# Batch 1's maximum and exponential moved into the first batch's FFN steps, with four small reorderings ahead of them

## The reference

```python
x = L0_attn_x                                   # (8, 512, 128) float32
x = x + _layernorm(_L0_attn_ref(_layernorm(x), gamma, beta, w_qkv, w_out, b_out))
x = x + _layernorm(_L0_ffn_ref(_layernorm(x), Wg, Wu, Wd))

# _L0_attn_ref: layernorm, q, k, v = xn @ w_qkv in 4 heads of 32
k = jax.nn.softmax(k, axis=1)                   # over the 512 tokens, per channel
context = jnp.einsum('bnhd,bnhe->bhde', k, v)
out = jnp.einsum('bhde,bnhd->bnhe', context, q * DIM_HEAD ** -0.5)
return out.reshape(b, n, 128) @ w_out + b_out + x

# _L0_ffn_ref: the sum over 8 experts, with hidden size 512
acc += (silu(x @ wg) * (x @ wu)) @ wd
```

## Time and profile before

| | before |
|---|---|
| three runs | 546.48, 546.70, 546.71 us; median 546.7 |
| the profiled execution | 546.29 us |
| its span in the profile | 544.5 us |
| TensorE busy | 536.6 us, 99% of the span |
| VectorE, ScalarE, GpSimd busy | 443.0, 345.5, 163.4 us |
| TensorE clock granted in the front and in the first steps | 1.00 of full speed |

### The profile page before, as it was taken

The page is one execution under the profiler, slowest core; times in us unless marked ns, Lnnn a source line. Parts: engine busy times, 40 slices in busy tenths (PEclk is TensorE's granted clock), DMA queues, the critical chain, the costliest instruction groups (busy, mean ns, idle before and its releaser), DMA issues.

```text
span 544.5 us, 8689 instructions
## 1 busy us (share of the span) xinstructions
PE 536.6 (99%) x2596; PEld 462.0 (85%) x2596; DVE 443.0 (81%) x987; ACT 345.5 (63%) x630; POOL 163.4 (30%) x211
## 2 busy tenths in 40 slices
PE   9899999999999999999999999999999999999996
PEld 5688888888888888888888888888888888888885
DVE  6796986989778897798978898688986889778666
ACT  5886877556675566755667566665667555655554
POOL 5697770305303171032601235021350005001001
PEclk9999999999999999999999999999999999999999
DMA  7254110220111201202012021020210210110000
GB/s 217 79 156 134 41 58 1 78 77 21 60 39 41 96 6 54 67 11 98 27 32 78 17 82 59 0 79 31 67 39 1 78 59 1 39 40 1 20 1 19
DMA packets 34081, 28.68 MB, mean 53 GB/s; under 512 B 3697, under 2 KB 25970, under 8 KB 34034
## 3 DMA queue, kind: packets, MB, share of 16 engines
q1 hardware_dynamic: 32736, 27.47, 15.9%
q10 hardware_dynamic: 1298, 0.66, 0.4%
HBM read 17.37 MB, written 10.75 MB: 52 GB/s over the span
## 4 chain that ended last, share of the span: by engine, by line
PE 97%; DVE 1%; DMA 0%; POOL 0%; issue 0%; SPq 0%; POOLq 0%; DVEq 0%; ACT 0%
PE acc_att_ps L1180 11%; PE acc_att_ps L1183 11%; PE acc_att_ps L1181 11%; PE gate_ps L1180 10%; PE gate_ps L1183 10%; PE gate_ps L1181 10%; PE up_ps L1180 10%; PE up_ps L1183 10%; PE up_ps L1181 10%; PE acc_att_ps L1226 1%; DMA wqkv<-in_L_attn_w_qkv_dram 0%; PE acc_att_ps L1214 0%; PE acc_att_ps L1234 0%; PE acc_att_ps L1335 0%; PE gate_ps L1415 0%
## 5 line engine op out<-in xcount | busy, mean ns | idle before, releaser
L715 ACT ACTIVATE gs<-gate_ps 128x512 f32<-128x512 f32 x255 | 152.0, 596 | 173.9 <-PE gate_ps L1183 171.6
L973 DVE TENSOR_TENSOR h<-gs,up_ps 128x512 f32<-128x512 f32 x231 | 157.7, 683 | 81.7 <-PE up_ps L1183 79.1
L960 DVE TENSOR_TENSOR h_lo<-h,h_hi 128x512 fp32r<-128x512 f32 x231 | 172.7, 748 | 0.2
L692 ACT ACTIVATE h_hi<-h 128x512 fp32r<-128x512 f32 x231 | 143.9, 623 | 7.7 <-DVE h L973 7.2
L1180 PE MATMUL gate_ps<-x1nT_hi,wg_hi 128*128 128x512 f32 (+1 forms) x254 | 98.0, 386 | 0.0
L1183 PE MATMUL acc_att_ps<-h_lo,wd_hi 128*128 128x512 f32 (+1 forms) x256 | 96.9, 379 | 0.0
L1180 PE MATMUL acc_att_ps<-h_hi,wd_hi 128*128 128x512 f32 (+1 forms) x256 | 96.9, 379 | 0.0
L1181 PE MATMUL acc_att_ps<-h_hi,wd_lo 128*128 128x512 f32 (+1 forms) x256 | 96.8, 378 | 0.0
L1180 PE MATMUL up_ps<-x1nT_hi,wu_hi 128*128 128x512 f32 (+1 forms) x254 | 96.2, 379 | 0.0
L1181 PE MATMUL up_ps<-x1nT_hi,wu_lo 128*128 128x512 f32 (+1 forms) x254 | 96.1, 378 | 0.0
L1181 PE MATMUL gate_ps<-x1nT_hi,wg_lo 128*128 128x512 f32 (+1 forms) x254 | 96.1, 378 | 0.0
(11 more groups left out here) (246 smaller groups left out, 535.4 us busy)
## 6 DMA issues: line engine op xcount, KB each, us to landing
w_raw<-in_L_ffn_Wg_dram SPq DMA_DIRECT2D x8, 256.0 KB, 3.1
w_raw<-in_L_ffn_Wu_dram SPq DMA_DIRECT2D x8, 256.0 KB, 3.0
w_raw<-in_L_ffn_Wd_dram SPq DMA_DIRECT2D x8, 256.0 KB, 2.9
x_in<-in_L_attn_x_dram SPq DMA_DIRECT2D x7, 256.0 KB, 2.9
t_dram_x1n<-t_blk_x1n SPq DMA_DIRECT2D x7, 256.0 KB, 2.0
t_out_x1n<-t_dram_x1n SPq DMA_DIRECT2D x28, 64.0 KB, 2.0
t_dram_acc<-t_blk_acc SPq DMA_DIRECT2D x7, 256.0 KB, 2.3
t_out_acc<-t_dram_acc SPq DMA_DIRECT2D x28, 64.0 KB, 2.0
```

The source lines that it names most:

```text
L692: act.activation(h_hi[s % NH][:, :], h_of(t, s)[:, :], ACT.Copy).then_inc(s_hhi, 1)
L715: act.activation(gs[q][:, :], gate_ps[q][:, :], ACT.Silu).then_inc(s_silu, 1)
L960: dve.tensor_tensor(h_lo[s % NH][:, :], h_of(t, s)[:, :], h_hi[s % NH][:, :].bitcast(F32), ALU.subtract).then_inc(s_hlo, 1)
L973: dve.tensor_tensor(h_of(t, s)[:, :], gs[q][:, :], up_ps[q][:, :], ALU.mult).then_inc(s_h, 1)
```

## The change

Five edits, all in the front and in batch 0's steps:

1. VectorE's `kmax` of batch 1 moves from the front to the beginning of step 3, and ScalarE's `exp` to the end of step 4. `E_T` and `E_store` follow one step later each, and the weight splits of steps 3 to 6 are moved out of the way: `split_hi(6)` into the front, `split_hi(8)` from step 5 to step 7 and those up to m = 17 one or two steps later than before; `split_lo` follows.
2. The load of silu's table moves ahead of `first_n(1)`'s copy in the front. As the exponential now stands in step 4, the program gains two loads there: exp's ahead of it and silu's behind it.
3. TensorE makes the second half's transposes (`first_n(1)`) before the first `early_low`, not after it.
4. `b_out`'s product moves from between `first_kT` and `first_k` to behind A, and takes 128 rows (a row of b_out and 127 of zeros that a new memset on VectorE writes) in place of one. VectorE's `kmax_diag` no longer waits for it; `first_yb(0)` does, and stands behind the copy of A.
5. `first_U(2)` moves ahead of `first_kT`.

```diff
-FIRST_DVE = {"E_T": 4, "next_stats": 8, "A": 12, "M": 14, "z": 17, "z_stats": 17, "next_T": 19, "wk_lo": 20,
+FIRST_DVE = {"kmax": 3, "E_T": 5, "next_stats": 8, "A": 12, "M": 14, "z": 17, "z_stats": 17, "next_T": 19, "wk_lo": 20,
-FIRST_ACT = {"E_store": 5, "E_load": 8, "G": 16, "wk_hi": 18, "next_xnT": 26, "next_xnT_hi": 27, "x1n_hi": 30}
+FIRST_ACT = {"exp": 4, "E_store": 6, "E_load": 8, "G": 16, "wk_hi": 18, "next_xnT": 26, "next_xnT_hi": 27, "x1n_hi": 30}
-HI_AT = {6: 2, 7: 3, 8: 5, 9: 6, 10: 7, 11: 8, 12: 9, 13: 11, 14: 12, 15: 13, 16: 14, 17: 15, 18: 17, 19: 18, 20: 19,
+HI_AT = {7: 2, 8: 7, 9: 8, 10: 9, 11: 10, 12: 11, 13: 12, 14: 13, 15: 14, 16: 15, 17: 16, 18: 17, 19: 18, 20: 19,
          21: 21, 22: 22, 23: 23}
-LO_AT = {5: 1, **{m: when + 1 for m, when in HI_AT.items()}}
+LO_AT = {5: 1, 6: 3, 7: 4, **{m: when + 1 for m, when in HI_AT.items() if m > 7}}
...
+        b_row = sb("b_row", [P, D])
...
+            act.wait_ge(s_b_zero, 1)
+            act.dma_start(b_row[0:1, :], b_out.rearrange("(a d) -> a d", a=1)).then_inc(s_b_row, 16)
...
-            act.wait_ge(s_f_erec, 1)
-            attention("exp", 1, 1, True)
+            act.wait_ge(s_mask, 3)
+            act.activation(silu_warm[:, :], zcol[:, :], ACT.Silu)
             act.wait_ge(s_f_n, 2)
             act.activation(blocks_of(x1nT_hi[0][:, :], 1), two(acc_ps[:, REST]), ACT.Copy).then_inc(s_x1nT_hi, 1)
-            act.wait_ge(s_mask, 3)
-            act.activation(silu_warm[:, :], zcol[:, :], ACT.Silu)
+            split_hi(6)
...
-            dve.wait_ge(s_bout_ps, 1)
...
+            dve.wait_ge(s_f_A_ps, 1)
+            dve.tensor_copy(A_sb[:, :], gate_ps[0][:, 0:D]).then_inc(s_f_A, 1)
+            dve.wait_ge(s_bout_ps, 1)
             dve.wait_ge(s_wvT, HEADS)
             first_yb(0)
-            dve.wait_ge(s_f_A_ps, 1)
-            dve.tensor_copy(A_sb[:, :], gate_ps[0][:, 0:D]).then_inc(s_f_A, 1)
...
-            dve.wait_ge(s_f_esum, 1)
-            attention("kmax", 1, 1, True)
...
+            first_U(2)
             pe.wait_ge(s_f_xnT, 1)
             first_kT(0, HALF)
...
-            pe.matmul(up_ps[2][:, D:2 * D], ones[0:1, :].bitcast(F32), b_row[:, :], start=True,
-                      stop=True).then_inc(s_bout_ps, 1)
...
-            first_U(2)
             first_U(3)
...
             last.then_inc(s_f_A_ps, 1)
+            pe.wait_ge(s_b_row, 16)
+            pe.wait_ge(s_U_half, 1)
+            pe.matmul(up_ps[2][:, D:2 * D], ones[:, :].bitcast(F32), b_row[:, :], start=True,
+                      stop=True).then_inc(s_bout_ps, 1)
...
             pe.wait_ge(s_f_lo, 1)
-            early_low(0, 0)
             first_n(1)
-            for s in range(1, EARLY):
+            for s in range(EARLY):
                 early_low(s, 0)
```

More of the change, by code:

```diff
@@ L111, in build @@
         bout_bc = sb("bout_bc", [P, D])
-        b_row = sb("b_row", [1, D])
+        b_row = sb("b_row", [P, D])
         wqkv = sb("wqkv", [P, 3 * D])
@@ L227, in build @@
         s_bout = sem("s_bout")
+        s_b_zero = sem("s_b_zero")
         s_b_row = sem("s_b_row")
@@ L654, in attention @@
                     if first:
+                        act.wait_ge(s_f_erec, 1)
                         act.activation(ET[:, :], att_ps[:, :], ACT.Exp, bias=kmax_neg[:, 0:1], scale=1.0,
@@ L725, in _ @@
             act.dma_start(bcol[:, :], beta[0].rearrange("a d -> d a")).then_inc(s_gb, 16)
-            act.dma_start(b_row[:, :], b_out.rearrange("(a d) -> a d", a=1)).then_inc(s_b_row, 16)
+            act.wait_ge(s_b_zero, 1)
+            act.dma_start(b_row[0:1, :], b_out.rearrange("(a d) -> a d", a=1)).then_inc(s_b_row, 16)
             act.wait_ge(s_w_ps, 1)
@@ L861, in attention @@
                     dve.wait_ge(s_kT_ps, c)
+                    if first:
+                        dve.wait_ge(s_f_esum, 1)
                     dve.tensor_reduce(kmax_neg[:, 0:1], att_ps[:, :], AX_X, ALU.max, negate=True).then_inc(s_kmax, 1)
@@ L997, in _ @@
             dve.memset(warm[:, :], 0.0).then_inc(s_warm, 1)
+            dve.memset(b_row[:, :], 0.0).then_inc(s_b_zero, 1)
             dve.memset(head_mask[:, :], 0.0).then_inc(s_mask, 1)
@@ L1359, in _ @@
             first_kT(1, REST)
-            pe.wait_ge(s_mask, 4)
-            pe.wait_ge(s_b_row, 16)
-            pe.wait_ge(s_U_half, 1)
-            pe.matmul(up_ps[2][:, D:2 * D], ones[0:1, :].bitcast(F32), b_row[:, :], start=True,
-                      stop=True).then_inc(s_bout_ps, 1)
             first_k(0)
             first_k(1)
+            pe.wait_ge(s_mask, 4)
             pe.wait_ge(s_f_kdiag, 1)
```

## The result

The changed kernel takes 549.55 us in the median of six runs (548.47 to 550.81), the kernel before beside it 546.59: a ratio of 1.0055 with an interval of 1.0036 to 1.0074. The forecast was 547.3, at most 548.1. The runs of the changed kernel stand in two groups, three near 548.5 and three near 550.6. The profiled run is one of the first group: 548.51 us, with a span of 546.7 against 544.5.

A forecast was written before the change was run, and what follows sets the result against it. TensorE, busy 99% of the span, was taken as the bound. Terms -0.05, -0.22, -0.45, +0.75, +0.38 and +0.2 summed to +0.6 us: 546.9 on the profiled execution, 547.3 as median, range 546.0 to 548.1 (0.80).

The forecast's parts named there:

- the one that carries VectorE in step 4: Steps around batch 0's step 4: engines carried forward by row distances; waits of +0.75, +0.38 and +0.2 us followed.
- the one collision: VectorE's h_lo(1) against GpSimd's wd_lo: not side by side, so h_lo(1) runs 25.8 to 26.4, about 1.4 us.
- The front to `through_heads`: Front: quicker kmax_diag wins 0.25 us, b_out's product behind A costs 0.22, U's product 0.02; -0.05 in all.
- the product of 128 rows: b_out's product behind A in the front: taken as 0.22 us, the shape of A's, against 0.41 for one row.
- The second half's first product: End of the front: first_n(1)'s transposes come sooner, -0.22 us; this product moves from 21.23 to 20.96.
- Silu's table: Step 0: the load runs earlier, gs(0) starts at 21.82 instead of 22.60, the first step's waiting goes; -0.45 us.
- Step 7: TensorE at down(4): waits +0.75 us for h_hi(4), then +0.38 for h_lo(4) at the third product.
- Step 9: TensorE at up(9): waits +0.2 us for the bank that a late h_lo(6) frees.
- Each table load costing as much again: Rival, step 4's two loads: ScalarE runs empty around each, step 7's wait grows 2.6 us, 549.9 us; chance 0.03.
- The drain of about 1380 ns: Skill page's rule for step 4's loads: 2.8 us more in all, sum +3.4; not used, loads taken as 1.30.
- GpSimd late for up(12): Rival, step 10: wu_lo of expert 3 late, slack 0.2 us, +0.5 more, 547.8; chance 0.13 with larger step 7 waits.
- The hidden block: Rival, step 4: ScalarE's block hidden by an early h_lo(1) or greater slack; 546.0 to 546.5 us; chance 0.17.

The follow-up runs named there:

- e11: The kernel before, unchanged, run and traced again: 546.53 us, span 544.7.
- e16: The changed kernel, unchanged, for a third trace: 547.93 us, one run.
- e4: Changed kernel with batch 1's maximum back in the front on VectorE, only the exponential in step 4: 547.49 us, ratio 1.0019.
- e2: Changed kernel with GpSimd's wg_lo split for expert 2 one step later, waiting for h_lo(3) instead of h_lo(2): 548.03 us, ratio 1.003.
- e3: Changed kernel with Identity for Exp in step 4, so no table loads there; batch 1's exponential left out: 546.23 us, ratio 0.9996.
- e9: Changed kernel with the exponential at the end of step 5 and a one-column memset (filler) on VectorE behind h_lo(4): 547.1 us, ratio 1.0005.
- e10: Changed kernel with the exponential at the end of step 5, no filler memset: 547.56 us, ratio 1.0014.
- e6: Changed kernel with a ready one-column memset (filler) on VectorE behind h_lo(3): 548.25 us, ratio 1.0041.
- e15: Changed kernel with GpSimd's yb moved behind the next wd_lo and batch 2's statistics one step later on VectorE: 549.48 us, ratio 1.0047.
- e8: Kernel before with only the move of the maximum and exponential, the step tables and split_hi(6): 549.48 us, ratio 1.0059.
- e13: e12 with the one-column memset (filler) on VectorE behind h_lo(4): 550.42 us, one run.
- e14: The kernel of e6, unchanged, for a second trace: 548.73 us, ratio 1.0036.
- e7: Kernel before with only edits 3 to 5 (second half's turn, b_out's product, first_U(2)): 546.56 us, ratio 1.0012.
- e5: e3 with five further Identity activations into unused tiles, holding ScalarE 3.4 us without a load: 548.49 us, ratio 1.0038.
- e1: The changed kernel, unchanged, run and traced again: 547.96 us, ratio 1.0035.
- e12: e10 with two Identity activations of 128x512 into idle tiles ahead of the exponential: 552.02 us, one run.

## Why the prediction was wrong

**The step that failed** is the one that carries VectorE in step 4: "I carry the engines forward with distances from rows", with `h_lo(1)` as the one collision and every later `h_lo` at its own length. The collision of `h_lo(3)` with three GpSimd instructions in a row has no term in the sum. Where `h_lo(3)` is passed over it costs 2.14 us of TensorE's waiting in step 6, and often 1.8 us of halved clock behind it. The waits that I had forecast for steps 7 and 9 are hidden behind it, so that the net price is smaller: by step 12 the first trace is 1.75 us behind e11 and e16, let in, 0.96. Passing over alone is thus worth 0.8 us and the clock 1.8. The two together fit the first set's groups at 548.5 and 550.6 (only one run of the first was traced). They were not among the rivals: the one that gave GpSimd the blame had it late for up(12), and its price was 0.5.

In the kernel before, `h_lo(3)` stood ahead of `wg_lo` (29.09 and 29.29), and it was `wg_lo` that waited. The rows of the kernel before, VectorE's and GpSimd's:

```profile
29.09 0.77 DVE L960 TENSOR_TENSOR h_lo<-h,h_hi 128x512 fp32r<-128x512 f32 x1
```

```profile
29.29 1.72 POOL L367 TENSOR_TENSOR wg_lo<-w_raw,wg_hi 128x512 fp32r<-128x512 f32 x1
```

The change turns that round by little, from 0.20 ahead to 0.24 behind: both engines are some 0.5 us earlier by the gains ahead of them, and the maximum in step 3 takes 0.61 us of VectorE between `h_lo(1)` and `h(3)`. e4, with all edits but the maximum's move, has `h_lo(3)` back in front (by 0.20) and no wait over 0.4 us in its one traced run. e2 turns the order round from GpSimd's side, with the same effect. But being behind `wg_lo` is not enough to lose: e3, e9 and e10 are behind it by 0.22 to 0.23 us too and were let in, and so were e6, e15 and e16.

**The terms, in a run where `h_lo(3)` is let in** (e16, laid beside e11; x arrives in both within 0.03 us). The front to `through_heads`: -0.06 (11.81 against 11.87 in the chains; forecast -0.05). That it comes out is luck: `kmax_diag` stands at 8.68 and in e11 at 8.69, so it had not waited for b_out's product. What is won is at `first_k_less_max`, 0.42 (9.17 against 9.59) where I had 0.25; A's products, 1.07 us in the chain in place of 0.89, give 0.18 of it back. Behind A the product of 128 rows takes the 0.22 us that I took for it. The second half's first product: 21.21 against 21.42, so -0.21 in all where I had -0.27. Silu's table: the first product of gate(4) stands at 25.25 against 25.92, so -0.67 in all and -0.46 for this term (forecast -0.45); the waiting of the first step is gone. Step 7: 33.27 - 32.16 is 0.89 more than the distance of two products (0.22), the product behind it comes 0.07 late, and the third and the one behind that 0.26 and 0.11: 1.33, where I had 0.75 + 0.38 = 1.13. Step 9: 0.17 + 0.10 = 0.27, where I had 0.2. The sum is -0.67 + 1.60 = +0.93, against a forecast of +0.6, and by step 12 e16 is 0.96 behind e11. Of the difference 0.21 is the first wait of step 7 (0.89 + 0.07, where I had 0.75), most of it the 0.14 behind `h_hi(3)`. The spans differ by 1.4 (546.1 and 544.7). Some 0.2 of the rest comes near step 118, in e16 and e10 alone. The other 0.29 comes near 290 us, far behind all edits, and goes with the program: VectorE's `h` of one step starts 1.06 us behind the end of its last product there and not 0.71, in all eleven traces of kernels with the edits 3 to 5 and without a filler; the two traces of the kernel before, e8 and the four with a filler (e6, e9, e13, e14) do not have it. e16's row and e11's:

```profile
290.70 0.69 DVE L979 TENSOR_TENSOR h<-gs,up_ps 128x512 f32<-128x512 f32 x1 [2.98 <-issue]
```

```profile
289.25 0.69 DVE L973 TENSOR_TENSOR h<-gs,up_ps 128x512 f32<-128x512 f32 x1 [2.62 <-PE up_ps L1183]
```

So the change costs these 0.29 too, which had no term in the sum, and it takes away all that the edits 3 to 5 win in e7. Its cause is open: no wait that the trace shows holds this `h`.

**The rivals.** Each table load costing as much again: it would have given 549.9, near the measured 549.55, and it is false. Both loads are 1.28 us with 0.02 on either side, and e5 has the passed-over `h_lo(3)` and the 2.2 us of waiting without a load. The drain of about 1380 ns that the page "ScalarE: Activation LUTs" of the Trainium skill states (section What ACT_TABLE_LOAD costs) is in none of these traces: behind the first 10 us no load in any of the eighteen starts more than 0.02 us behind the activation ahead of it. GpSimd late for up(12): it was on the edge. In e16 `wu_lo` ends at 43.57 and its first product starts at 43.96; in e15, with `yb` in the way, GpSimd's chain moves 1.9 us and TensorE waits:

```profile
44.16 1.27 POOL L369 TENSOR_TENSOR wu_lo<-w_raw,wu_hi 128x512 fp32r<-128x512 f32 x1
```

```profile
45.48 0.48 PE L1184 MATMUL up_ps<-x1nT_hi,wu_hi 128*128 128x512 f32 x1 [1.48 <-POOL wu_lo L369]
```

The hidden block: not seen; where nothing is passed over the block costs the 1.6 us of waits in steps 7 and 9 (e16; e3, without the loads, has none of them), and 1.3 in e4 against e3 (547.49 and 546.23), which differ by the maximum's place too.

**What stays open** is what decides whether VectorE gets in. Among the traces in which `h_lo(3)` is issued 0.2 to 0.3 us behind `wg_lo`, seven show 4.04 or 4.05 us and six show 1.59 or 1.60. Neither what stands behind it nor a table load tells them apart, and the same kernel shows both (e1 and e16, e6 and e14). One row goes with the outcome: `h_lo(2)`, two instructions ahead of it, takes 0.69 or 0.70 us in all seven that are passed over and 0.68 in five of the six that are let in (0.70 and 0.68 at 27.87 in the first trace and e16); the sixth, e6, has 0.70. So hundredths of a microsecond in how the two engines meet may decide; I saw this only afterwards and no run tests it.

A rival stands beside it: the runs were on several chips, and, as far as the chips are recorded, no kernel was traced twice on one. The three traces of e12 to e14 (one chip) are passed over, the two of e9 and e10 and the two of e15 and e16 (one chip each) let in; the other two chips show both, but in different kernels. Whether it is drawn in each execution or goes with the chip or the kernel is therefore not shown. Nor is how long the passing lasts: all seven have the same three instructions, and e15, with two, was let in. Going by e16's 547.93, the five runs of e1 between 547.77 and 548.07 may be runs in which it was let in, and none of the first set's six; but they have no traces. e3 has ten of eleven runs below 546.5, so by its times it is hardly ever passed over there.

The page "SBUF — State Buffer" of the Trainium skill, section SBUF: two separate sides, says that GpSimd and a VectorE operation with two inputs in SBUF share a pair of ports as an exclusive lock, and that whichever starts first holds it for its whole instruction. These traces agree: `h_lo(3)` ends 0.55 or 0.56 us behind the end of a GpSimd instruction in all thirteen. Who gets the lock next, the traces show to be either.

No version here beats the kernel before beyond what can be measured: the best that computes everything is e7 at 546.56 (e9 has 1.0005), and even without the exponential's loads 546.23 is within it.

## What to carry to other kernels

When you move work on one engine, list for each of its instructions what a neighbour that excludes it has in its queue at that moment, and give the collision a range up to the neighbour's whole uninterrupted row, not the price of one instruction: here 3 x 1.26 us, where the order of two instructions had turned by 0.44 us. Keeping the 0.2 us by which VectorE went first before was worth more than the 0.7 us won in the front, and a wait of some 2 us on TensorE may cost nearly twice its length, as the clock can fall behind it. Look at the single times, not at the median alone: groups of them say that something varies from one execution to the next, and then one trace that fits a theory is no proof of it. And lay the whole program beside the old one: 0.29 us of this change's cost stands near 290 us, far behind the last edit.

## What I had not expected of the hardware

- A VectorE instruction of 0.68 us took 4.04 us, since three GpSimd instructions of 1.26 us each went ahead of it; in another run of the same program, on another chip, it took 1.60.
- TensorE's clock fell to 1.2 GHz for 3.4 us behind a wait of 2.1 to 2.2 us in the middle of full work, in five traces of seven.
- Two things outside the program shift the whole of it. x's first part is there between 2.96 and 3.25 us, in the unchanged kernel too (2.97 and 3.16). And TensorE's full clock (1.00 of 2.4 GHz) is recorded from 3.7 us on in e1 and only from 9.1 us on in e12 (4.2 in the kernel before, whose front was not all at 1.00 either); the front comes 0.6 us late in e2 (from 6.9 us) and 1.8 in e12.
- One `h` of VectorE near 290 us starts 0.35 us later in the programs with edits 3 to 5 and no filler, though nothing in its surroundings was edited.
